# A fused adaLN attention block with two feed-forward layers: the ternary stage's second half begun inside the first half's second layer, and the gate of y split by feature half

## What is computed

```python
def _L0_cond_ref(x, timestep_embed, ...):            # 16 heads of 128
    ada = (timestep_embed @ ada_w + ada_b)[:, None, :]
    shift1, scale1, gate1, shift2, scale2, gate2 = jnp.split(ada, 6, axis=-1)
    x1 = _ln(x) * (1.0 + scale1) + shift1
    qkv = (x1 @ qkv_w + qkv_b).reshape(Bc, Tc, 3, H, DH)
    attn = softmax(q k^T * DH ** -0.5)
    attn_out = (attn v) @ out_w + out_b
    x = x + gate1 * attn_out
    x2 = _ln(x) * (1.0 + scale2) + shift2
    h = jax.nn.gelu(x2 @ ffn_w1 + ffn_b1, approximate=False)
    return x + gate2 * (h @ ffn_w2 + ffn_b2)

def _L0_ffn_ref(x, W_fc, W_proj):                    # weights made ternary first
    h = jnp.square(jax.nn.relu(jnp.einsum('bsd,hd->bsh', x, w1)))
    hn = _rms_norm(h)
    return jnp.einsum('bsh,dh->bsd', hn, w2)

# result: x + _L0_ffn_ref(_L0_cond_ref(x, cond, ...), W_fc, W_proj)
```

## Time and profile before

| | |
|---|---|
| three runs | 350.14 us median, 349.57 to 350.66 |
| profiled execution | 350.69 us, of which 348.9 us span |
| TensorE busy | 342.3 us, 98% of the span |
| VectorE, ScalarE, GpSimd busy | 222.4, 220.2, 148.7 us |
| granted TensorE clock, mean | 0.996 |
| DMA | 16.53 MB, 47 GB/s on average |

### The profile page before, as it was taken

One profiled execution on the slowest core, in us unless ns is written; L12 is line 12 of the kernel. 1 busy time (PEld: TensorE's weight loads), 2 busy tenths in 40 slices (PEclk: granted clock), 3 DMA queues, 4 the chain that ended last, 5 costly groups with the idle time before them and its releaser, 6 DMA issues.

```text
span 348.9 us, 5879 instructions
## 1 busy us (share of the span) xinstructions
PE 342.3 (98%) x1950; PEld 293.7 (84%) x1950; DVE 222.4 (64%) x386; ACT 220.2 (63%) x560; POOL 148.7 (43%) x140
## 2 busy tenths in 40 slices
PE   8999999999999999999999999999999999999995
PEld 7888888889888888888888888888787788889884
DVE  6676756553555664456466454585875788577796
ACT  2773565667576657756664675667579536876593
POOL 3571329736534964644595573479341100000000
PEclk9999999999999999999999999999999999999998
DMA  6953003100300320030020002020000000000002
GB/s 176 362 192 120 3 0 120 62 1 3 120 0 0 120 60 0 0 120 0 25 95 0 0 6 115 0 62 0 4 0 2 0 2 0 0 2 1 1 32 90
DMA packets 12338, 16.53 MB, mean 47 GB/s; under 512 B 720, under 2 KB 8992, under 8 KB 12320
## 3 DMA queue, kind: packets, MB, share of 16 engines
q1 hardware_dynamic: 12136, 16.16, 14.2%
q10 hardware_dynamic: 184, 0.15, 0.1%
HBM read 15.25 MB, written 1.05 MB: 47 GB/s over the span
## 4 chain that ended last, share of the span: by engine, by line
PE 74%; issue 20%; DVE 3%; ACT 1%; POOL 1%; POOLq 0%; ACTq 0%
PE bank L1228 16%; PE bank L1230 16%; PE bank L1229 16%; PE bank L1315 8%; PE bank L1298 8%; PE bank L1304 4%; PE bank L1427 2%; PE bank L1442 1%; DVE yT L976 1%; DVE yT L966 1%; PE bank L1463 1%; PE bank L1422 1%; DVE yT L962 0%; ACT prob L579 0%; ACT hbuf L718 0%
## 5 line engine op out<-in xcount | busy, mean ns | idle before, releaser
L391 POOL TENSOR_TENSOR prob<-prob,rinv 128x512 f32<-128x512 f32 x32 | 36.2, 1131 | 60.3 <-DVE rinv L1025 59.9
L579 ACT ACTIVATE prob<-bank,negmax 128x128 f32<-128x128 f32 x128 | 45.4, 365 | 25.6 <-DVE negmax L1012 25.6
L1315 PEld LDWEIGHTS bank<-probT,vals 128*128 128x128 f32 x256 | 33.3, 191 | 3.2 <-issue 0.8
L952 DVE SCALAR_TENSOR_TENSOR o_lo<-bank,bias,o_hi 128x512 fp32r<-128x512 f32 x32 | 23.9, 745 | 17.2 <-ACT o_hi L532 17.2
L532 ACT ACTIVATE o_hi<-bank,bias 128x512 fp32r<-128x512 f32 x32 | 21.9, 686 | 19.4 <-PE bank L1315 19.4
L1315 PE MATMUL bank<-probT,vals 128*128 128x128 f32 x256 | 33.9, 275 | 0.0
L350 POOL TENSOR_TENSOR wqk_lo<-raw_qk,wqk_hi 128x512 fp32r<-128x512 f32 x16 | 21.2, 1323 | 19.6 <-ACT wqk_hi L493 18.1
L488 POOL TENSOR_TENSOR xr<-raw_qk,xt 128x256 f32<-128x256 f32 x1 | 0.7, 721 | 67.2 <-ACT raw_qk L796 67.2
L1012 DVE TENSOR_REDUCE negmax<-bank 128x4 f32<-128x512 f32 x32 | 21.8, 682 | 7.9 <-PE bank L1298 7.9
L1228 PE MATMUL bank<-wv_hi,x_hi 128*128 128x512 f32 x62 | 26.1, 420 | 0.0
L579 ACT ACTIVATION_READ_ACCUMULATOR prob<-bank,negmax 128x1 f32 x128 | 26.0, 203 | 0.0
(11 more groups left out here) (218 smaller groups left out, 974.1 us busy)
## 6 DMA issues: line engine op xcount, KB each, us to landing
raw_qk<-in_L_cond_qkv_w_dram SPq DMA_DIRECT2D x6, 512.0 KB, 4.6
raw_v<-in_L_cond_qkv_w_dram SPq DMA_DIRECT2D x4, 512.0 KB, 4.1
raw_o<-in_L_cond_out_w_dram SPq DMA_DIRECT2D x4, 512.0 KB, 3.5
t_w<-in_L_cond_ada_w_dram SPq DMA_DIRECT2D x1, 1024.0 KB, 8.9
raw_w<-in_L_cond_ffn_w_dram SPq DMA_DIRECT2D x2, 512.0 KB, 6.9
t_raw<-in_L_ffn_W_fc_dram SPq DMA_DIRECT2D x4, 256.0 KB, 3.7
t_raw<-in_L_ffn_W_proj_dram SPq DMA_DIRECT2D x4, 256.0 KB, 3.8
raw_qk<-in_L_cond_ffn_w_dram SPq DMA_DIRECT2D x1, 1024.0 KB, 4.9
```

Source lines behind the costliest of these rows:

```text
L391: nc.gpsimd.tensor_tensor(e, e, rinv[:, j % 2, :].unsqueeze(2).broadcast_to([P, SQ, P]), ALU.mult).then_inc(norm_done, 1)
L579: e = nc.scalar.activation(prob[:, j % 2, s, :], bank[BS][:, s * P:(s + 1) * P], ACT.Exp, bias=negmax[:, j % 2, s:s + 1], accum_out=rowsum ...
L952: nc.vector.scalar_tensor_tensor(out=lo[:, :], in0=bank[BO][:, :], scalar=bias[:, bass.ds(HG * G + VB + j % HG, 1)], in1=hi[:, :].bitcast( ...
L1315: m = nc.tensor.matmul(bank[BO][:, s * P:(s + 1) * P], vals[:, b, h], probT[:, s, :], start=True, stop=True)
```

## The change

Five edits, all of order; no arithmetic is added or taken away.

- `gate_y` keeps the two products with the gate; the two additions of x become `add_x`. Each addition now signals for itself, and `transpose_y` goes feature block by feature block and waits for one addition at a time. Half 0 calls both at the same place as before.
- In the first half's feed-forward layer one, VectorE has `gate_y(1)` behind the low part of chunk 2, `add_x(1)` behind that of chunk 3, and the statistics behind that of chunk 6. TensorE's `transpose_y(1)` moves behind chunk 6, ahead of `transpose_fc`.
- In the first half's ternary stage, VectorE has both gates of the second half's x ahead of the square of chunk 6 and both residuals behind the low part of chunk 5. On ScalarE the high parts of this x go ahead of chunk 7's.
- TensorE stops the first half's `ternary2` after six chunks and does `ternary1(1, 0)`, `ternary2(0, 6)`, `ternary1(1, 1)`, `ternary2(0, 7)`, `ternary1(1, 2)`, and `sum_squares(0)` behind chunk 2 of the second half instead of chunk 0.
- To go with that, `square_root(0)` on ScalarE and `row_scale(0)`, `finish(0)` and `finish(1)` on VectorE each move one chunk down in the second half's loop.

```diff
@@ ScalarE
-            def ternary_hidden(quad, c, between=None):
+            def ternary_hidden(quad, c):
 ...
-                ternary_hidden(0, c, between=(lambda: x3_hi(1)) if c == NC - 1 else None)
+                if c == NC - 1:
+                    x3_hi(1)
+                ternary_hidden(0, c)
 ...
-                if c == 0:
+                if c == 1:
                     square_root(0)
@@ VectorE
+            def add_x(quad):
                 dve.wait_ge(xT_done, quad + 1)
                 for c in range(KD):
                     dve.wait_ge(gate_mul, KD * quad + c + 1)
-                    m = nc.vector.tensor_tensor(yT[:, c, cols(quad)], yT[:, c, cols(quad)], xT[:, c, cols(quad)], ALU.add)
-                m.then_inc(gated, 1)
+                    nc.vector.tensor_tensor(yT[:, c, cols(quad)], yT[:, c, cols(quad)], xT[:, c, cols(quad)], ALU.add).then_inc(gated, 1)
 ...
                     gate_y(0)
+                    add_x(0)
 ...
-                        dve.wait_ge(gated, quad + 1)
+                        dve.wait_ge(gated, KD * (quad + 1))
 ...
                     accumulate(NU - 1, NG - 1, 1, last=True)
+                if c == 2:
                     gate_y(1)
-                if c == 5:
+                if c == 3:
+                    add_x(1)
+                if c == 6:
                     dve.wait_ge(gt_mm, 2)
                     stats_of(3)
 ...
-            for c in range(NC):
+            for c in range(NC - 2):
                 ternary_r(0, c)
-                if c == NC - 1:
-                    residual0()
-                    residual1()
-                if c == NC - 2:
-                    gate0()
                 if c:
                     ternary_r_lo(0, c - 1)
-                if c == NC - 2:
-                    gate1()
-                if 2 <= c < NC - 1:
+                if c >= 2:
                     add_squares(0, c - 1)
+            gate0()
+            gate1()
+            ternary_r(0, NC - 2)
+            ternary_r_lo(0, NC - 3)
+            residual0()
+            residual1()
+            ternary_r(0, NC - 1)
+            ternary_r_lo(0, NC - 2)
+            add_squares(0, NC - 3)
+            split_lo(1, KD * 5)
             ternary_r_lo(0, NC - 1)
-            split_lo(1, KD * 5)
             add_squares(0, NC - 2)
+            ternary_r(1, 0)
             add_squares(0, NC - 1)
-            for c in range(NC):
+            for c in range(1, NC):
 ...
-                if c == 1:
+                if c == 2:
                     row_scale(0)
-                if c in (2, 3):
-                    finish(c - 2)
+                if c in (3, 4):
+                    finish(c - 3)
@@ TensorE
-                pe.wait_ge(gated, quad + 1)
-                for s in range(SQ):
-                    for c in range(KD):
+                for c in range(KD):
+                    pe.wait_ge(gated, KD * quad + c + 1)
+                    for s in range(SQ):
 ...
-                if c == 5:
+                if c == 6:
                     pe.wait_ge(xT_done, 2)
                     transpose_y(1)
-                if c == 6:
                     pe.wait_ge(t_done, NG)
 ...
-            for c in range(NC):
+            LAG = 3
+            for c in range(NC - 2):
                 ternary2(0, c, range(SQ))
             pe.wait_ge(xs_lo, 6 * KD)
-            pe.wait_ge(ones_set, 1)
-            LAG = 3
             for c in range(NC):
                 ternary1(1, c)
-                if c == 0:
+                if c < 2:
+                    ternary2(0, NC - 2 + c, range(SQ))
+                if c == 2:
+                    pe.wait_ge(ones_set, 1)
                     sum_squares(0)
```

More of the change, by code:

```diff
@@ L768, in ternary_hidden @@
                 hi_part(hidden(quad, c)[0], hbuf[:, n % 2, :], r_h)
-                if between:
-                    between()
                 if c:
@@ L1186, in _ @@
             gate0, gate1, residual0, residual1 = x3_steps(1)
-            for c in range(NC):
+            for c in range(NC - 2):
                 ternary_r(0, c)
-                if c == NC - 1:
-                    residual0()
-                    residual1()
-                if c == NC - 2:
-                    gate0()
                 if c:
                     ternary_r_lo(0, c - 1)
-                if c == NC - 2:
-                    gate1()
-                if 2 <= c < NC - 1:
+                if c >= 2:
                     add_squares(0, c - 1)
+            gate0()
[8 more added lines that the diff above has]
+            split_lo(1, KD * 5)
             ternary_r_lo(0, NC - 1)
-            split_lo(1, KD * 5)
             add_squares(0, NC - 2)
+            ternary_r(1, 0)
             add_squares(0, NC - 1)
-            for c in range(NC):
+            for c in range(1, NC):
                 if c not in ON_SCALAR:
                     ternary_r(1, c)
-                if c:
-                    ternary_r_lo(1, c - 1)
+                ternary_r_lo(1, c - 1)
                 if c >= 2:
                     add_squares(1, c - 1)
-                if c == 1:
+                if c == 2:
                     row_scale(0)
-                if c in (2, 3):
-                    finish(c - 2)
+                if c in (3, 4):
+                    finish(c - 3)
             add_squares(1, NC - 1)
```

## The result

The median after is 348.82 us (348.52 to 349.12) against 350.14 before (349.48 to 350.66): ratio 0.9964, 95% interval 0.9953 to 0.9974, so 0.9 to 1.6 us faster. Seven executions of each kernel were timed; one of the changed kernel's seven was slow, at 687.93 us, and range and interval leave it out. The forecast was 349.0.

The account below looks back on a forecast made before the run. TensorE, busy 98% of the span, was taken to bound the kernel, so only its waits mattered. Gains of 0.05 + 0.83 + 0.2 = 1.1 us gave 349.0 us against the 350.14 median, range 347.4 to 350.3.

Parts of the forecast that it names:

- Part 1: First half's y transposes: 0.40 us wait filled, but the output product waits for o_lo, so 0.05 us gained.
- Part 2: Second half's y inside feed-forward layer one: wait for chunk 4's Gelu filled, layer two 0.83 us sooner.
- The slack behind the normalisation: Second half's normalisation ends at 280.7, TensorE wants it at 281.21; 0.5 us remains.
- The rival that part 2 gives nothing: Gap at 271 filled, but normalisation or copies behind it late by as much; 349.9 us, chance 0.20.
- Part 3: Turn between ternary-stage halves: 1.9 us earlier start, mostly spent waiting for finish 1; 0.2 us gained.
- The chain of times: Ternary stage's steps timed from 318.42: finish 1 done at 335.9, last sum of squares at 343.1.
- The sum: Whole kernel: gains of 0.05, 0.83 and 0.2 make 1.1 us, giving 349.0 us against the median.
- The rival without a wait: Ternary stage: no wait for finish 1, early turn all kept; 2.6 us in sum, 347.6 us, chance 0.18.
- The rival of the falling clock: TensorE's clock halves in the wait for finish 1; 2.4 us slower in sum, 352.5 us, chance 0.12.

Follow-up runs that it names:

- ffn_only: Kernel before with y's gate and additions split and the first half's feed-forward layer one reordered, ternary stage as it was; 349.26 us, ratio 0.9976.
- The two half steps: Kernel before with y split, plus feed-forward layer one's new order on VectorE only (350.54 us) or y's transposes moved on TensorE only (350.78 us).
- turn_only: Kernel before with the edits of the ternary stage alone; 350.02 us, ratio 0.9999.
- clock_gap: Changed kernel with finish(1) moved behind chunk 4's low part and sum and two unused VectorE additions, lengthening TensorE's wait; 353.78 us, ratio 1.0111.
- fin_both_c3: Changed kernel with finish(1) directly behind finish(0), before the square of chunk 4; 347.52 us, ratio 0.9932.

## Why the prediction was right

**Part 1, 0.05:** 0.05 in the trace, by the step named: the freed 0.40 turns into a wait for o_lo. A time of 0.05 can't be told in a measurement, and part 1 wasn't run by itself, so this rests on the trace alone.

**Part 2, 0.83:** 0.81 in the trace. The difference of medians in ffn_only is 0.79, with part 1 in it. Each step came as worked out: layer two at 275.73 with the old start-up (275.7 said), no wait at 271 to 273, statistics in time for the normalisation. The slack behind the normalisation is 0.3 (280.27 to 280.57), for the 0.5 said. The rival that part 2 gives nothing is refuted by ffn_only. The two half steps show why the sum had to be made over three engines: neither order gains by itself, since each removes one of the two things that TensorE was waiting for and exposes the other.

**Part 3, 0.2:** 0.10. The chain of times held step by step. With the 1.47 by which the stage's start had moved added back, first 3 ends at 330.67 (330.65 said), and finish 1 is done at 333.96 + 0.47 + 1.47 = 335.90 (335.9 said). TensorE stands for 1.5, as said, when it is counted as the prediction counted it, from start to start: the next matmul could have started at 333.04 (332.92 + 0.12) and did at 334.49, 1.45 later. The bracket's 1.29 leaves out the rest of the last matmul's length. The last sum starts at 343.23, said 343.1. Nearly all of these 0.13 is there when first 7 ends, at 338.11 + 1.47 = 339.58 for 339.46: the matmuls behind the wait took a little longer than summed, and ScalarE's and VectorE's squares behind them kept to the plan.

**The sum** of 1.1 stands against 0.97 in the trace (1.57 less the start-up's 0.60) and 1.32 in the medians, whose interval of 0.9 to 1.6 holds both. The 0.35 between trace and medians is within the interval. Measured by themselves, the two edits of ffn_only and turn_only add up to 0.79 + 0.03 = 0.82.

**The rival without a wait** was false for this kernel and right in its price: it put the last sum at 341.6 and the time at 347.6. With the finishes together the sum starts at 341.70 on the old clock (340.57, the start moved by 1.13) and the time is 347.52.

**The rival of the falling clock** was false for a wait of 1.3: the stretches around the wait show 1.00 in the profiled execution, and the six executions compared lie within 0.6 of each other with a mean clock of 0.996 or more, which leaves no room for a fall that costs 1.5. It was not far off: at 2.7 it came true in 5 of 12 executions and at 3.9 in all. Its reason, that the clock drops some 0.8 us after the last matmul, held for the one trace that it was read from and doesn't carry over. In clock_gap the clock was still 1.00 when the matmuls began again, 3.9 us on. And at the end of fin_both_c3, where the last matmul ends at 342.68, it falls only at 345.7, 3.0 us later (busy time of TensorE by stretches):
```profile
342.50:343.00 0.50, 0.18 (x2) 1.00 0.83 275
343.00:345.00 2.00, 0.00 (x0) 1.00 0.78 260
345.00:345.50 0.50, 0.00 (x0) 1.00 0.57 189
345.50:346.00 0.50, 0.00 (x0) 0.72 0.00 0
```
Its price, 3.5 us of loss for work at half clock, was too high for the profiled execution of clock_gap: 1.54 was measured, since the clock came back before that work was done. For three of the six it was nearly right: they are 3.1 above the 351.38 without a fall (median 354.50), the other three 1.6 (353.02). The Trainium skill, "TensorE: Matmul & The Clock Gate", section "HAM oscillation — how this bites in real kernels", has a TensorE that idles too long start its next burst slow. The trace of clock_gap agrees for 3.9 us, but for the burst's first 0.5 us, which was still at 1.00; that of the changed kernel shows no such thing for 1.3.

## What to carry to other kernels

An instruction that frees a buffer (here a small one that reads a bank) belongs by the time when the bank is asked for, not by the chunk to which its data belongs: when the asking engine is moved sooner, move every such reader with it. Here this one line decided whether a reordering of three engines gave 0.1 or 1.6 us.

Where two engines wait on each other through a third, a move on one of them alone may cost time and the pair gain it, so test the pair before the parts are given up. A wait that a plan leaves on TensorE can have a second price beyond its length, here in some executions at 2.7 us and in all at 3.9.

## What the runs showed of the hardware

The clock's fall is not certain at a given length of the wait: none seen at 1.3 us, 5 of 12 executions at 2.7, 6 of 6 at 3.9 (by time and mean clock; one fall was profiled). In that profile it comes late, 0.5 us after the matmuls had begun again, and costs 1.54 us. In clock_gap the six runs form two groups, 352.81 to 353.27 with a mean clock of 0.995 and 354.29 to 354.58 with 0.990, some 1.6 and 3.1 above the time without a fall, so a second fall or a longer one is possible; only one of the first group was profiled, so what the others did stays open. After the kernel's last matmul the clock fell after 0.8 us before and after 3.0 in fin_both_c3, so one such delay says little about another kernel.

The start-up differs from execution to execution by up to 1.35 us (first layer-norm transposes at 8.52 to 9.87), which is more than the whole effect of this change. Two single profiles are compared by distances inside a stage, not by their spans.
